# An audio-tower kernel: the first slot names inside the last attention, a new order of the work between the last attention and the experts

## The reference, cut to what matters

```python
# 1 token mixing: depthwise convolution (7 taps), 192x192 product, relu, max over pairs of
#   tokens (1024 -> 512), real part of a 2-D Fourier transform, LayerNorm, gamma, beta
h = _L0_tok_ref(x, ...)                                   # [4, 512, 192]
# 2 linear attention, 12 heads of 16, second-order Taylor features, causal:
h = h + _L0_attn_ref(_layernorm(h), Wq, Wk, Wv, Wo)
# 3 mixture of 8 experts, one expert for a token (x = _layernorm(h)):
probs = softmax(x @ Wg + bg); top_p = max(probs); comb = one_hot(argmax(probs)) * top_p
y = gelu(x @ W1[e] + b1[e]) @ W2[e] + b2[e]               # 192 -> 768 -> 192
ffn_out = y of the chosen expert * top_p
v = clip(ffn_out @ Wv + bv, -3, 3)
scores = sigmoid(x @ Wm + bm); mask = scores >= the 204th highest of the batch
gr, gi = diagonal of the inverse of a tridiagonal matrix with diagonal v  # recursions over 512 tokens
h = h + ffn_out + bk_scale * (clip([gr, gi] * mask, -10, 10) @ Wo + bo)
```

## Time and profile before

| | us |
|---|---|
| median of 3 runs | 442.24 |
| lowest, highest of them | 436.63, 442.59 |
| the profiled execution: its own time | 429.96 |
| its span | 428.2 |
| what lies around the span | 1.76 |
| busy in the span: PE, DVE, ACT, POOL | 373.9, 271.1, 150.1, 91.2 |

### The profile page before, as it was taken

The page is one execution under the profiler, slowest core; times in us unless marked ns, Lnnn a source line. Parts: engine busy times, 40 slices in busy tenths (PEclk is TensorE's granted clock), DMA queues, the critical chain, the costliest instruction groups (busy, mean ns, idle before and its releaser), DMA issues.

```text
span 428.2 us, 7994 instructions
## 1 busy us (share of the span) xinstructions
PE 373.9 (87%) x2820; PEld 265.8 (62%) x2821; DVE 271.1 (63%) x866; ACT 150.1 (35%) x299; POOL 91.2 (21%) x128
## 2 busy tenths in 40 slices
PE   7999899889898888988988997889799999998273
PEld 4486657436374354743665535689699899887252
DVE  6689703999198992987024386738556655565783
ACT  1010120773106732067434461354333443342000
POOL 1000000451003520034101241400634433341100
PEclk9999899999899999999996899969999999999656
DMA  8667120000300000086002001120241111113504
GB/s 269 196 215 263 44 55 0 2 2 2 100 0 2 1 2 2 0 331 210 2 2 86 2 2 73 51 61 2 83 141 43 53 45 51 46 51 56 165 3 147
DMA packets 21571, 30.58 MB, mean 71 GB/s; under 512 B 9876, under 2 KB 18132, under 8 KB 21028
## 3 DMA queue, kind: packets, MB, share of 16 engines
q1 hardware_dynamic: 17812, 24.02, 17.5%
q0 software_dynamic: 2208, 5.29, 4.3%
q10 hardware_dynamic: 1520, 0.86, 0.7%
HBM read 24.20 MB, written 5.96 MB: 70 GB/s over the span
## 4 chain that ended last, share of the span: by engine, by line
PE 66%; DVE 14%; ACT 7%; issue 5%; DMA 3%; POOL 3%; DVEq 0%; ACTq 0%; POOLq 0%
PE upper L1630 10%; PE ring L1616 7%; PE upper L1479 5%; PE ring L1463 4%; PE ring L1620 4%; ACT probs L639 4%; PE ring L1372 4%; POOL probs L569 3%; PE upper L1307 2%; PE ring L1378 2%; PE ring L1353 2%; PE ring L1319 2%; PE upper L1535 2%; PE upper L1396 2%; PE ring L1358 2%
## 5 line engine op out<-in xcount | busy, mean ns | idle before, releaser
L569 POOL TENSOR_SCALAR_AFFINE_SELECT probs<-probs 128x256 f32<-128x256 f32 (+1 forms) x72 | 43.4, 604 | 212.9 <-ACT probs L639 211.8
L639 ACT ACTIVATE probs<-ring,ones 128x768 f32<-128x768 f32 (+1 forms) x54 | 52.0, 995 | 23.3 <-PE ring L1463 16.9
L721 ACT ACTIVATE probs<-ring,qk 128x128 f32<-128x128 f32 x138 | 38.2, 378 | 55.4 <-PE ring L1620 30.2
L1630 PE MATMUL upper<-w,probs 128*128 x276 | 51.8, 339 | 3.1 <-DVE probs L1105 1.8
L1630 PEld LDWEIGHTS upper<-w,probs 128*128 128x128 f32 x276 | 46.1, 196 | 5.2 <-issue 4.9
L1479 PE MATMUL upper<-probs,va 128*32 128x512 f32 (+3 forms) x384 | 34.9, 459 | 12.6 <-POOL probs L569 12.6
L1463 PE MATMUL ring<-qk 32*128 32x512 f32 (+3 forms) x276 | 43.0, 520 | 3.1 <-ACT probs L639 3.1
L770 DVE SCALAR_TENSOR_TENSOR wide<-w,wdw,wide 128x512 f32<-128x512 f32 (+1 forms) x42 | 41.1, 1020 | 0.6
L585 POOL DMA_INDIRECT ffn_by_token<-probs,target x23 | 22.5, 979 | 72.3 <-DVE probs L1113 71.1
L1616 PE MATMUL ring<-xsT,qk 128*128 128x128 f32 x276 | 35.9, 280 | 0.6 <-ACT xsT L713 0.6
L1463 PEld LDWEIGHTS ring<-qk 32*128 32x128 f32 x276 | 19.9, 193 | 25.3 <-ACT probs L639 18.9
(11 more groups left out here) (324 smaller groups left out, 624.7 us busy)
## 6 DMA issues: line engine op xcount, KB each, us to landing
w<-in_w SPq DMA_DIRECT2D x1, 4608.0 KB, 15.8
w1a<-in_w1a SPq DMA_DIRECT2D x1, 3072.0 KB, 10.5
w<-in_x SPq DMA_DIRECT2D x4, 512.0 KB, 3.9
w<-in_x SPq DMA_DIRECT2D x8, 256.0 KB, 5.0
w1b<-in_w1b SPq DMA_DIRECT2D x1, 1536.0 KB, 13.8
tokens<-x_all SPq DMA_DIRECT2D x4, 384.0 KB, 8.7
x_all<-ffn_by_token SPq DMA_DIRECT2D x4, 384.0 KB, 5.0
wide<-scores_linear SPq DMA_DIRECT2D x1, 1024.0 KB, 5.3
```

The source lines that it names most:

```text
L569: nc.gpsimd.affine_select(diag, diag, heads + [[1, P]], ALU.is_ge, minus_one, base=0, channel_multiplier=-1).then_inc(p_ready, 1)
L639: nc.scalar.activation(squares(n), score_bank(b, n)[:, :, 0:unit_width(n)], ACT.Square, bias=ones[:, 0:1], scale=0.25).then_inc(sq_done, 1)
L721: nc.scalar.activation(hT[slot][:, c, :], ring[slot][:, c % 2, P * (c // 2):P * (c // 2) + P], ACT.Gelu_apprx_tanh, bias=b1_col[slot][:, c ...
L1630: last = nc.tensor.matmul(att[2][:, 0:D], hT[slot][:, c, :], w2[:, bass.ds((e * HC + c) * D, D)], start=(c == 0), stop=(c == HC - 1))
```

## The change

Six edits, all between the start of the last attention and the fifth slot tile.

1. TensorE in the last attention: `turn_third(0)` and `turn_third(1)` one pair of units earlier (n = 0 and 2), `logits(2)` at n = 4, `count(0)` at n = 6, and `name_slots(0)` inside it, after the scores of units 16, 17 and ahead of `values(14)` and `values(16)`.
2. VectorE in the last attention: after `name_tiles(0)` come `take_names(0)`, `fetch_w1(0)` and `fetch_w1(1)`, and only then `sums(3, 2)`. The big comparison of `spell` (L1008) is cut into pieces of four tiles.
3. TensorE after the attention: both `keep_clock` calls are gone; `turn_attended(3)`, `turn_back(3)` (now into `ring[1]`), `turn_slots(0)` (bank `misc`), `turn_slots(1)` (bank `att[2]`), `output(3)`, `up(0)`, `turn(3)`, `up(1)`, `turn_slots(2)`, `down(0)`, `turn_slots(3)`, `logits(3)`, `down(1)`, the first half of `up(2)`, `count(1)`, its second half, `turn_slots(4)`, `up(3)`, `down(2)`, `name_slots(1)`, `up(4)`, `down(3)`.
4. The slot buffers `xs` move from `probs` into `xT`, so that the gathers wait for `v_done` and no longer for the end of the last attention. GpSimd's order becomes five gathers, `gather(5)`, `store_slots(0)`, `store_slots(1)`, `store_slots(2)`, `gather(6)`, and on as before.
5. ScalarE and VectorE follow TensorE's order: ScalarE copies batch 3's transposes (`turned(3)`) between gelu of tile 0 and gelu of tile 1; VectorE takes tiles 0, 1 and 2 out at other places.
6. `layernorm` gets a parameter `ahead_of_last`, a function to call before its last four instructions. No caller passes one.

```diff
-        xs = [probs[:, at + ROW * i:at + ROW * i + ROW] for i in range(2)]
-        at += 2 * ROW
+        xs = [xT[:, ROW * i:ROW * i + ROW] for i in range(2)]
...
-            pool.wait_ge(av_done, NU * B)
+            pool.wait_ge(v_done, B)
...
             for i in range(SURE):
                 gather(i)
+            pool.wait_ge(s_rows_out[B - 1], 32)
+            gather(SURE)
             store_slots(0)
             store_slots(1)
-            pool.wait_ge(s_rows_out[B - 1], 32)
-            gather(SURE)
             store_slots(2)
             gather(SURE + 1)
...
-            copy_slots(0, 0, att[2])
-            copy_slots(1, 1)
+            turned_back(B - 1)
+            copy_slots(0, 0, misc)
+            copy_slots(1, 1, att[2])
             gelu(0, 0)
+            turned(B - 1)
+            gelu(1, 1)
             copy_slots(2, 0)
-            gelu(1, 1)
-            turned(B - 1)
             copy_slots(3, 1)
...
                     sums(b, 1)
                     name_tiles(0)
+                    take_names(0)
+                    dve.wait_ge(s_w1a, 16)
+                    dve.wait_ge(s_w1b, 16)
+                    dve.wait_ge(te_ready, 1)
+                    dve.wait_ge(s_done, NU * B)
+                    fetch_w1(0, 0)
+                    fetch_w1(1, 1)
                     sums(b, 2)
...
-                st.mark(V.tensor_tensor(one_hot(n), over(mx[:, tiles], P), every(slot_ids[:], P), ALU.is_equal))
+                for i in range(0, nt, NT):
+                    at = mx[:, tiles.start + i:tiles.start + i + NT]
+                    st.mark(V.tensor_tensor(one_hot(n)[:, i:i + NT, :], at[:, :, None].to_broadcast([P, NT, P]),
+                                            slot_ids[:, None, :].to_broadcast([P, NT, P]), ALU.is_equal))
...
             divide(B - 1)
-            take_names(0)
-            dve.wait_ge(s_w1b, 16)
-            fetch_w1(0, 0)
-            fetch_w1(1, 1)
             add_attended(B - 1)
+            dve.wait_ge(s_w2, 32)
             normalise_again(B - 1)
             fetch_w1(2, 0)
+            take_out(0)
             fetch_w1(3, 1)
             choose(1)
-            dve.wait_ge(s_w2, 32)
-            take_out(0)
+            take_out(1)
             place(1)
             spell(1)
-            take_out(1)
             fetch_w1(4, 0)
             take_names(1)
+            take_out(2)
+            name_tiles(1)
             weigh_out(0)
             weigh_out(1)
-            name_tiles(1)
-            take_out(2)
             weigh_out(2)
             fetch_w1(5, 1)
...
-                    if b == B - 1 and n in (2, 4):
-                        turn_third(n // 2 - 1)
-                    if b == B - 1 and n == 6:
+                    if b == B - 1 and n in (0, 2):
+                        turn_third(n // 2)
+                    if b == B - 1 and n == 4:
                         pe.wait_ge(third_copied, 2)
                         pe.wait_ge(pt_copied, B)
                         logits(2)
-                    if b == B - 1 and n == 8:
+                    if b == B - 1 and n == 6:
                         count(0)
+                    if b == B - 1 and n == 16:
+                        name_slots(0)
...
             pe.wait_ge(sq_done, NU * B)
-            keep_clock(8, ring[1][:, 0, :])
             turn_attended(B - 1)
-            name_slots(0)
             turn_back(B - 1)
-            keep_clock(6, ring[1][:, 0, :])
-            output(B - 1)
...
-            turn_slots(0, 0, 1, att[2])
+            turn_slots(0, 0, 1, misc)
+            turn_slots(1, 1, 1, att[2])
+            output(B - 1)
+            up(0, 0)
+            turn(B - 1)
+            up(1, 1)
             pe.wait_ge(attn_added, B)
-            turn_slots(1, 1, 1)
-            up(0, 0)
-            up(1, 1)
             turn_slots(2, 0, 2)
-            turn(B - 1)
+            pe.wait_ge(te_ready, 1)
+            pe.wait_ge(s_w2, 32)
+            down(0, 0)
             turn_slots(3, 1, 2)
             pe.wait_ge(t2_copied, B - 1)
             logits(B - 1)
-            down(0, 0)
+            down(1, 1)
+            up_long(2, 0)
             count(1)
-            up(2, 0)
-            down(1, 1)
+            up_short(0)
             turn_slots(4, 0, 3)
             up(3, 1)
+            down(2, 0)
             name_slots(1)
-            down(2, 0)
             up(4, 0)
             down(3, 1)
```

More of the change, by code:

```diff
@@ L129, in turn_bank, with back_ring @@
             return ring[b % 2] if b < B - 1 else ring[0]
-        back_bank = ring[0][:, :, :].rearrange("p c n -> p (c n)")[:, 0:N + N // 2]
+        def back_ring(b):
+            return ring[0] if b < B - 1 else ring[1]
         ring4 = [r[:, :, :].rearrange("p a (b n) -> p (a b) n", b=2) for r in ring]
@@ L707, in _ @@
             order(front, project, attend)
-            turned_back(B - 1)
             def copy_slots(i, slot, bank=None):
@@ L919, in _, with fetch_w1, take_out @@
             width = [E * (tiles.stop - tiles.start) for tiles in PASSES]
+            def fetch_w1(i, slot):
+                e = dve.value_load(te_i[0:1, bass.ds(i, 1)], min_val=0, max_val=E - 1)
+                ahead(dve, up_done, i - 1)
+                V.tensor_copy(w1_wide[slot], w1a[:, bass.ds(e * HID, HID)]).then_inc(w1_fetched, 1)
+                V.tensor_copy(w1_pair[slot], w1b[:, bass.ds(e * (HID // 2), HID // 2)]).then_inc(w1_fetched, 1)
+                ahead(dve, gelu_done, HC * (i - 1))
+                V.tensor_copy(b1_col[slot], b1t[:, bass.ds(e * HC, HC)]).then_inc(w1_fetched, 1)
+            def take_out(i):
+                e = dve.value_load(te_i[0:1, bass.ds(i, 1)], min_val=0, max_val=E - 1)
+                ahead(dve, s_ys[i % 4], stores_before(i, i % 4))
+                dve.wait_ge(dn_done, i + 1)
+                V.tensor_tensor(ys[i % 4][:, 0:D], att[2][:, 0:D], b2[:, bass.ds(e * D, D)], ALU.add
+                                ).then_inc(ys_copied, 1)
             def choose(n):
@@ L1084, in _ @@
             order(front, project, attend)
-            def fetch_w1(i, slot):
-                e = dve.value_load(te_i[0:1, bass.ds(i, 1)], min_val=0, max_val=E - 1)
-                ahead(dve, up_done, i - 1)
-                V.tensor_copy(w1_wide[slot], w1a[:, bass.ds(e * HID, HID)]).then_inc(w1_fetched, 1)
-                V.tensor_copy(w1_pair[slot], w1b[:, bass.ds(e * (HID // 2), HID // 2)]).then_inc(w1_fetched, 1)
-                ahead(dve, gelu_done, HC * (i - 1))
-                V.tensor_copy(b1_col[slot], b1t[:, bass.ds(e * HC, HC)]).then_inc(w1_fetched, 1)
             def count_higher(i):
@@ L1438, in turn_back @@
                 pe.wait_ge(o_ready, HG * (b + 1))
-                turned_chunks(ring[0], att_tok, back_done)
+                turned_chunks(back_ring(b), att_tok, back_done)
             def output(b):
@@ L1512, in turn, with name_slots @@
                 last.then_inc(t2_done, 1)
+            def name_slots(n):
+                pe.wait_ge(spelled, n + 1)
+                hot, say = one_hot(n), spelling(n)
+                count = PASSES[n].stop - PASSES[n].start
+                for i in range(count):
+                    last = nc.tensor.matmul(named, hot[:, i, :], say[:, i, :], start=(i == 0), stop=(i == count - 1))
+                last.then_inc(names_done, 1)
             def turn_third(c):
@@ L1584, in _ @@
                     project(b + 1)
-            def name_slots(n):
-                pe.wait_ge(spelled, n + 1)
-                hot, say = one_hot(n), spelling(n)
-                count = PASSES[n].stop - PASSES[n].start
-                for i in range(count):
-                    last = nc.tensor.matmul(named, hot[:, i, :], say[:, i, :], start=(i == 0), stop=(i == count - 1))
-                last.then_inc(names_done, 1)
-            pe.wait_ge(sq_done, NU * B)
-            keep_clock(8, ring[1][:, 0, :])
-            turn_attended(B - 1)
-            name_slots(0)
-            turn_back(B - 1)
-            keep_clock(6, ring[1][:, 0, :])
-            output(B - 1)
             def turn_slots(i, slot, loads, bank=None):
@@ L1607, in turn_slots, with up_banks, up_long @@
                 nc.tensor.transpose(bank[:, P:2 * P], xs[slot][:, P:2 * P], ident[:]).then_inc(xst_done, 1)
-            def up(i, slot):
+            def up_banks(slot):
+                return [ring[slot][:, c % 2, P * (c // 2):P * (c // 2) + P] for c in range(HC)]
+            def up_long(i, slot):
                 pe.wait_ge(w1_fetched, 3 * i + 2)
@@ L1613, in up @@
                 ahead(pe, gelu_done, HC * (i - 1))
-                out = [ring[slot][:, c % 2, P * (c // 2):P * (c // 2) + P] for c in range(HC)]
+                out = up_banks(slot)
                 for c in range(HC):
@@ L1617, in up, with up_short @@
                                      start=(c < 2), stop=False)
+            def up_short(slot):
+                out = up_banks(slot)
                 for c in range(HC):
@@ L1622, in up @@
                 last.then_inc(up_done, 1)
```

(3 more changed lines are left out.)

25 lines of the change are left out of this document (10 added, 15 removed).

## The result

The changed kernel takes 442.12 us as the median of four runs (439.42 to 449.24), the kernel before 439.44 beside it (433.03 to 442.59). The comparison that leaves disturbed runs out gives a ratio of **1.0181**, interval 1.0115 to 1.0247: slower by 1.1 to 2.5%, some 8 us. The profiled execution took 440.67 us, and its span is 438.9 against 428.2.

What follows compares the result with a forecast made beforehand. The prediction took TensorE, 66% of the chain, as the bound, so the start of up(6) decides. Queue terms of +2.7 us and the clock's +2.3 gave +5.0 on a median of 442.24: 447.2 us, range 439 to 453.

Steps and rivals of the forecast that it cites:

- the clock: TensorE without the two keep_clock calls: half rate at one of two places for part of its length, +2.3 us.
- place(0): VectorE in the last attention: its start gains 0 from the earlier logits, at most 1.4 us.
- name_slots(0) ahead of the values: TensorE, end of last attention: 2.78 us of names delay the last two values, 0.6 us, covered by the next step.
- names and fetches ahead of the last sum: VectorE, end of last attention: sums(3, 2) ends at 265.8, 3.2 us later, range 2.4 to 3.6.
- turn_back free of the names: TensorE after the attention: turn_back no longer waits for the names, a gain of 0.6 us.
- turn(3) ahead of up(1): TensorE at batch 3's LayerNorm: idle about 4 us, more work ahead of the logits, place(1) 3.6 us later.
- pass 1: From place(1): source rows after 9.0 us, gather(6) behind three stores, up(6) at 313.9 against 311.2.
- one sign that I named: TensorE was to stand idle ahead of the turn of slot tile 6, gather(6) being behind three stores.
- Rival A: TensorE's clock holds, only queue terms of +1 to +3.5 us are left: 444.5 us; chance 0.24.
- Rival C: Both clock drops, half rate from 265 over most of the way to count(1), +10.7 us: 453; chance 0.13.
- Rival B: Faster: VectorE's chain starts earlier than granted, -2 to -3 us: 439.5 us; chance 0.16.
- Rival D: The change doesn't do what it says, or an unseen wait cancels it: 442 us; chance 0.07.

Runs made afterwards that it cites:

- e1: The changed kernel with fillers (products of zeros) put back in four idle places of TensorE, up to batch 3's transposes; ratio 1.0105 to the kernel before.
- e7: The changed kernel with fillers ahead of the names and the two turnings, and up(1) back ahead of batch 3's transposes; ratio 1.0064 to the kernel before.
- e3: The changed kernel with up(1) back ahead of batch 3's transposes, ScalarE's order following; ratio 1.0162 to the kernel before.
- e4: The changed kernel with pass 0's names behind turn_attended and VectorE's last sum ahead of names and W1 fetches, no fillers; ratio 1.0244 to the kernel before.
- e6: The kernel before without its two runs of fillers at the end of the last attention, nothing else; ratio 1.0003.
- e2: The changed kernel with VectorE's last sum ahead of the first names and two W1 fetches, which go behind divide; ratio 1.0465 to the kernel before.
- e10: The kernel before with the gathers of tiles 5 and 6 ahead of the first three stores, nothing else; ratio 1.0018.
- e9: The kernel before with pass 0 one pair of units earlier and the gathers of tiles 5 and 6 ahead of the first three stores; ratio 0.9985.
- e12: The changed kernel with names, W1 fetches, turn_slots and up(1) back in the old order, two fillers, and gather(6) ahead of the stores; ratio 0.998 to the kernel before.

## Why the prediction was right, and where it was off

The direction and the two places were right, and the size fits: +5.0 us, between 439 and 453, forecast 447; measured 442.1, with 439.4 beside it for the kernel before. In the stretch itself the profile shows +7.6 and the timed ratio some 8 us. That the sum came so near is partly luck: the clock cost 4 us more than forecast, `up(5)` came 2.2 us later, and against them stood a gain of 2.3 that I had put at nothing, with smaller terms of 1.4 together. Term by term, from the first scores:

- *place(0)*: taken at 0, range to 1.4 earlier. Measured 2.8 us earlier (15.5 against 18.3), 2.3 at the spelling's end. I misread my own rows: before, `place(0)` waited for the count, and now it waits for `sums(3, 0)`, which waits for `values(4)`. Their end moves from 244.4 by 1.1 us, and the sum's 0.7 us behind it give 244.0 against 246.84, so 2.8 was in the rows. With the scores at half rate it was near 0, as I had said: in the experiments that have this edit the gain was 0.3 to 2.8.
- *name_slots(0) ahead of the values*: priced at 2.78 + 1.7 us and as covered. Measured 5.36 + 2.79. I let the clock fall after 263; it fell between 258 and 260, behind the 2.72 us that TensorE stood idle ahead of the names, and that wait was in my own text. In e1 and e7, with fillers there and 0.97 us idle, it held.
- *names and fetches ahead of the last sum*: 3.2 us from the end of the spelling. Measured 6.0 (27.95 to 37.74, against 30.21 to 34.04), of it 2.4 the wait for the half-rate names; with the clock held (e1) 3.3 more than before: the term holds at full rate.
- *turn_back free of the names*: 0.6 expected. At full rate (e1) 3.2 us from turning to turning back against 4.0: 0.8. At half rate it vanished (4.5).
- *turn(3) ahead of up(1)*: idle 4 us, measured 3.96. The logits were expected at 57.8 and came at 61.2, 1.7 of it because the LayerNorm was later. From the LayerNorm to the logits it took 7.9 us where 6.2 was forecast: 5.7 at full rate (e1), and 2.2 for the half rate. The order alone costs 2.2 of the 5.7 (e7: 3.6).
- *pass 1*: 9.0 us to the source rows, measured 8.8; `gather(6)` 7.3 after them, measured 7.2. But `up(5)` came 8.2 us after the source rows, not 5.8. ScalarE's late copy is 1.7 of it, which I had no row for, and `up(4)` at half rate had already held the turning of tile 5 (14.5 us behind `place(1)`, 12.9 in e7, where `up(4)` took 1.6). For the same reason one sign that I named did not come: TensorE did not stand idle ahead of the turning of tile 6. It did in e3 and e4.
- *the clock*: taken at one drop, +2.3, range 0 to 8. There were two drops up to the logits, which e1 prices at 6.3 us. This is the term that was mis-sized most.

The queue terms at full rate can be summed from e1 as well: from the spelling to the LayerNorm +2.5, forecast +2.6, and from there to the logits +1.8, forecast +2.3. From the logits to `place(1)` the changed kernel was 1.7 us shorter than before.

Rival A (the clock holds) is refuted by the windows. Rival C's mechanism, both drops, is what happened, at 6.3 us where it had 8; the total stayed under its +10.7 because the spelling ended 2.3 us earlier. Rival B's mechanism did happen too (the earlier spelling) and was eaten behind it; its condition, `sums(3, 2)` ending before 263, did not come (268.6). Rival D's 442 is the measured median only by the accident that the kernel before read 439.4 this time: the ratio's interval leaves out 1.

The rule of the Trainium skill, "TensorE: Matmul & The Clock Gate", Part 1, as the prediction uses it, named both drops, and the windows show them (0.50 from 260 to 268 and from 284 to 288). The price that the prediction put beside it, some +8 us in all, doesn't follow from its own terms, which give 2.7 + 8 = 10.7 as in rival C. And by e6 (1.0003) missing filler alone costs nothing here that can be measured.

## What to carry to other kernels

Before work is pulled ahead on an in-order engine, ask what it stood beside: the W1 copies and names were free behind `divide`, and cost 3.3 us ahead of the last sum. Putting work into an engine's queue where it must wait for another engine (the names in the attention) opens a new idle time ahead of it. Here TensorE's clock fell behind that idle time, and what was queued behind took about twice as long. A group of reorderings can be one unit: undoing one of them (e2) was worse than all, because another relied on it. And when an edit is to be read from one profile of each kernel, count from the last point that both share: the same code ended its spelling at 28.0 and at 30.9 here.

## What the runs showed that I had not expected

- The half rate lies elsewhere from execution to execution, even where the code is the same. It lay at 284 to 288 alone in the kernel before, at 264 to 268 without fillers (e6, 1.0003), and at both places in e10, which has the fillers. It also came while TensorE was busy throughout, behind logits of 9 columns: the window 228 to 232 of the kernel before reads 0.50 after 4 us at a busy share of 1.

```profile
224.00:228.00 4.00, 4.00 (x37) 3.98 (x35) 3.55 (x21) 1.02 (x1) 0.00 (x0) 0.98 0.00 0
228.00:232.00 4.00, 3.01 (x14) 1.43 (x13) 1.54 (x6) 1.12 (x2) 0.00 (x0) 0.50 0.36 109
```

- The loop over slot tiles has two paces: 4.6 us from one `up` to the next in the kernel before, the changed one and others, 5.6 us in the executions of e1 and e9 and for the first tiles of e2, e10 and e12, with ScalarE waiting 1.6 us ahead of gelu for nothing that the profile shows. The chain of e1 has it once in each pair of tiles, which is one pass of ScalarE's loop, 11.3 us apart:

```profile
327.94 0.16 DVE qk L937
328.11 1.62 issue
329.73 0.20 ACT probs L720
```

  Over ten tiles that would be 10 us, as an estimate, more than most edits here; the timed runs of e1 lie up to 10.7 us apart (435.57 to 446.24). Whether this pace makes that difference is not shown, since each kernel has one profile.
